# Expert feed-forward loops of a three-stage block: W1 slices as the stationary operand, the first norm's variance from matrix products

## The chip, the cores and the metric

The kernel runs on one core of a Trainium2 chip. The metric is device time in microseconds (us) of one execution; the time before is the median of three runs. Engines are named as the profile names them: PE (TensorE, with PEld for its weight loads), DVE (VectorE), ACT (ScalarE), POOL (GpSimd) and SP (SyncE, which here only issues transfers).

## The reference, cut to what matters

The block is x + 0.5 FFN(norm x), then x + attention(norm x), then x + 0.5 FFN(norm x) again, for 2048 tokens of 128 features. The FFN has eight experts, of which each token takes two:

```
h = jnp.einsum('td,edf->etf', xt, W1) + b1[:, None, :]
h = _layernorm(jax.nn.relu(h), g1, be1)
y = jnp.einsum('etf,efd->etd', h, W2) + b2[:, None, :]
y = _layernorm(jax.nn.relu(y), g2, be2)
...
out = jnp.einsum('te,etd->td', gate, y)
```

W1 is 128 x 512 per expert and W2 512 x 128. Everything is fp32.

## The kernel before

The program has three stages, f1 (first FFN, 46 to 160 us of the profiled span), the attention (160 to 337 us) and f2 (second FFN, 337 to 446 us, its first seven pairs woven into the attention's end by a written order). In each FFN stage tokens are sorted by expert into 39 tiles of 128 rows; a tile has one expert. The expert loop works on pairs of tiles, 20 per stage, n being the pair and u = n % 2 its buffer.

For a pair, PE turns the gathered rows (`turn_x`, line 963), multiplies the turned x by W1 (`hidden`, line 974: x stationary, 512 columns of W1 moving, the expert's place a register), turns relu's result in eight transposes (`turn_h`, line 983), and multiplies by W2 (`second`, line 993: turned h stationary, 128 columns of W2 moving, eight products per pair). The profile shows two records for each fp32 product. ACT copies x out of PSUM (line 749), makes the relu into `hh` (line 756), copies the turned h into `hT` (line 762), takes the two norms' square roots (`sqrt1` 766, `sqrt2` 770) and writes the scaled rows (`finish`, 777). DVE takes the mean and variance of the 512 hidden values with `stats1` (1378) and `moments1` (1385); W2's columns are centred beforehand, so that only the variance of the first norm is needed. It then makes r1 (`y_scale`, 1391), scales y and adds the bias (`y_sums`, 1397), takes the second norm's statistics (`y_stats`, 1403 to 1409) and applies it (`y_norm`, 1419 and 1421, behind `sqrt2`).

Each engine runs its queue in the order in which the code is written, and semaphores tie the queues. In a body of PE, `turn_h(n)`, `turn_x(n+2)`, `hidden(n+1)`, `second(n)` follow one another. On DVE, the statistics of pair n+1 stand between `y_stats` and `y_norm` of pair n-1. Pairs 2 to 7 of f1 and 6 to 15 of f2 are hardware loops with two pairs in an iteration, at whose head the expert numbers are loaded into registers; the others are written out. Pairs 8 to 19 of f1 carry work of the attention beside them (`between`, `behind`): pairs 8 to 11 a shared-bias product each on PE (1109) and an add on DVE. In f1, SP stores each finished pair (379), and after every second pair an empty 1032 KB block for f2 (426); POOL gathers the rows. In f2, SP loads each tile's rows (413) and POOL scatters the results.

## Time and profile before

| what | value |
|---|---|
| median of 3 runs (lowest to highest) | 470.97 us (470.0 to 471.98) |
| profiled execution: its own time, its span | 471.78 us, 469.6 us |
| PE busy, PEld busy | 406.1 us (86%), 282.9 us (60%) |
| DVE busy, ACT busy, POOL busy | 348.0 us (74%), 289.3 us (62%), 245.3 us (52%) |
| granted TensorE clock, mean | 0.926 |
| f1 / attention / f2 with the combination (from where the stages begin) | 46 to 160, 160 to 337, 337 to 470 us |

The span is the time from the first to the last instruction of the core; the execution's own time is 2.2 us longer. Busy shares are means over stages that have different limits, so an engine's need is to be read inside one stage. A start-to-start distance in a timeline is what an instruction costs its engine; its own length is up to 0.15 us longer, since the next one begins before it has ended.

### The profile page before, as it was taken

The numbers are of one execution on the slowest core, as the hardware profiler recorded it, in microseconds if no ns is written. First come the engines' busy times: TensorE is split into PE (matmuls) and PEld (weight loads), VectorE is DVE, ScalarE is ACT, GpSimd is POOL, SyncE is SP. The second block draws the span as 40 slices with busy tenths as digits, with TensorE's granted clock in tenths as the row PEclk, the third lists the DMA queues.
The fourth block names the chain that finished last, engine by engine and source line by source line (L and its number), as shares of the span: only waits on it lengthen the run. The fifth ranks groups of instructions, "written<-read, shape, count | busy, mean of one in ns | idle before, by whom it ended". The sixth has DMA issues, their size and how long they took to land.

```text
span 469.6 us, 11623 instructions
## 1 busy us (share of the span) xinstructions
PE 406.1 (86%) x3573; PEld 282.9 (60%) x3574; DVE 348.0 (74%) x1297; ACT 289.3 (62%) x594; POOL 245.3 (52%) x348
## 2 busy tenths in 40 slices
PE   7699999999798767888888998877889499999985
PEld 7445578777576544546465665644467278787734
DVE  8666678877749883789688797855668768888865
ACT  3186786765467765777576777743756357667630
POOL 8873643443631155366556757556624647555540
PEclk9798999999979955999799999978999889999998
DMA  7910116544433310000001000001111121211027
GB/s 214 338 65 17 29 48 214 175 155 141 137 76 122 131 35 22 21 13 24 13 18 24 19 26 24 25 29 34 53 47 35 55 53 53 62 57 55 30 75 228
DMA packets 27444, 35.15 MB, mean 75 GB/s; under 512 B 4329, under 2 KB 20641, under 8 KB 26242
## 3 DMA queue, kind: packets, MB, share of 16 engines
q1 hardware_dynamic: 22450, 24.62, 15.9%
q0 software_dynamic: 4944, 9.90, 7.7%
q8 instruction: 27, 0.44, 0.4%
q14 instruction: 23, 0.19, 0.1%
HBM read 15.45 MB, written 18.24 MB: 72 GB/s over the span
## 4 chain that ended last, share of the span: by engine, by line
PE 52%; DVE 15%; issue 10%; POOL 7%; ACT 7%; DMA 4%; another core or an unknown queue 2%; DVEq 1%; SPq 1%; POOLq 0%; ACTq 0%
PE bank L993 10%; PE bank L974 10%; PE bank L983 5%; DVE mx L2152 4%; PE bank L1915 2%; PE bank L1183 2%; PE bank L1178 2%; ACT early L1726 2%; PE bank L1933 2%; PE bank L2369 2%; PE bank L1937 2%; PE bank L1866 1%; PE bank L1935 1%; POOL xr_scratch L461 1%
## 5 line engine op out<-in xcount | busy, mean ns | idle before, releaser
L993 PEld LDWEIGHTS bank<-w2c,hT 128*128 128x128 f32 x624 | 77.4, 197 | 30.2 <-issue 29.1
L993 PE MATMUL bank<-w2c,hT 128*128 x624 | 78.9, 281 | 10.9 <-ACT hT L762 10.7
L974 PE MATMUL bank<-w1s,xT 128*128 x156 | 75.8, 608 | 0.8 <-DVE w2c L2387 0.8
L2152 DVE TENSOR_REDUCE mx<-bank 128x4 f32<-128x1024 f32 (+1 forms) x48 | 58.4, 1220 | 21.2 <-PE bank L1875 18.8
L1726 ACT ACTIVATE early<-bank 128x768 f32<-128x768 f32 x64 | 51.9, 813 | 30.4 <-PE bank L1923 29.9
L1378 DVE BATCH_NORM_STATS2 st<-wide 128x6 f32<-128x512 f32 x78 | 50.1, 683 | 22.8 <-ACT wide L756 12.7
L515 POOL DMA_INDIRECT xgw<-xn_scratch,slot_u x39 | 37.2, 954 | 45.3 <-PE bank L963 27.7
L762 ACT COPY hT<-bank 128x1024 f32<-128x1024 f32 (+1 forms) x40 | 39.5, 988 | 34.4 <-PE bank L983 30.5
L581 POOL DMA_INDIRECT yk<-y_scratch,posi x32 | 32.0, 1000 | 47.3 <-PE bank L1923 20.7
L485 POOL DMA_INDIRECT y_scratch<-yo,dest_u x39 | 39.0, 999 | 33.5 <-PE bank L983 19.4
L756 ACT ACTIVATE wide<-bank 128x1024 f32<-128x1024 f32 (+1 forms) x40 | 40.1, 1001 | 16.5 <-remote 7.1
L461 POOL DMA_INDIRECT xr_scratch<-row_buf,hi_i x32 | 31.7, 990 | 31.3 <-PE bank L1923 19.6
L983 PE MATMUL bank<-ident,wide 128*128 128x128 f32 x312 | 40.8, 273 | 1.3 <-issue 1.2
L974 PEld LDWEIGHTS bank<-w1s,xT 128*128 128x128 f32 x156 | 27.6, 194 | 22.8 <-issue 22.7
L983 PEld LDWEIGHTS bank<-ident,wide 128*128 128x128 f32 x312 | 35.1, 141 | 2.3 <-issue 2.0
L1915 PE MATMUL bank<-mxT,sel 64*128 64x384 bf16 x128 | 22.9, 354 | 12.8 <-ACT early L1726 6.8
L1397 DVE SCALAR_TENSOR_TENSOR yy<-bank,r,b2p 128x128 f32<-128x128 f32 x78 | 24.6, 351 | 11.2 <-remote 5.1
L939 ACT COPY wide<-bank 128x1024 bf16<-128x1024 bf16 x28 | 28.4, 1015 | 5.2 <-PE bank L1183 2.6
L777 ACT ACTIVATE yo<-yz,r 128x128 f32<-128x128 f32 x78 | 27.1, 396 | 3.6 <-DVE yz L1421 2.9
L1866 PE MATMUL bank<-mrhs,mlhs 64*128 64x128 bf16 (+1 forms) x192 | 16.7, 256 | 11.9 <-DVE mx L2152 7.2
L1915 PEld LDWEIGHTS bank<-mxT,sel 64*128 64x128 bf16 x128 | 6.3, 94 | 32.2 <-ACT early L1726 13.8
L1421 DVE SCALAR_TENSOR_TENSOR yz<-yy,mv,g2b 128x128 f32<-128x128 f32 x78 | 23.4, 340 | 0.2 <-issue 0.2
(382 smaller groups left out, 907.2 us busy)
## 6 DMA issues: line engine op xcount, KB each, us to landing
xr_scratch<-row_buf SPq DMA_DIRECT2D x8, 1032.0 KB
xgw<-xr_scratch SPq DMA_DIRECT2D x39, 64.5 KB
y_scratch<-yo SPq DMA_DIRECT2D x19, 128.0 KB
w1s<-in_L_ffn_W_dram SPq DMA_DIRECT2D x1, 2048.0 KB, 8.5
early<-y_scratch SPq DMA_DIRECT2D x8, 256.0 KB, 3.8
xs<-in_L_attn_x_dram SPq DMA_DIRECT2D x4, 256.0 KB, 3.6
xn_scratch<-row_buf SPq DMA_DIRECT2D x1, 1024.0 KB
out_dram<-xs SPq DMA_DIRECT2D x8, 128.0 KB, 2.5
```

The costliest lines, as they stand in the source:

```text
L461: pool.indirect_dma_start(out=xr_dram, out_offset=bass.IndirectOffsetOnAxis(ap=slot2[:, c:c + 1], axis=0), in_=rows_of[t // HALF][:, t % H ...
L485: pool.indirect_dma_start(out=y_dram, out_offset=bass.IndirectOffsetOnAxis(ap=dest_u[:, 2 * p + j:2 * p + j + 1], axis=0), in_=yo[:, p % 2 ...
L515: pool.indirect_dma_start(out=xg[:, u, :], out_offset=None, in_=xn_dram, in_offset=bass.IndirectOffsetOnAxis(ap=slot_u[:, n:n + 1], axis=0 ...
L756: act.activation(hh[:, u, 0:k, :], banks[:, h_at[u]:h_at[u] + k, :], ACT.Relu).then_inc(S["relu"], 1)
L762: act.copy(hT[:, u, 0:k, :], banks[:, 5:5 + k, :]).then_inc(S["hTc"], 1)
L974: last = pe.matmul(bank[h_at[u] + j][:], xT[:, u, j, :], w1s[:, bass.ds(e * FF, FF)], start=True, stop=True)
L983: last = pe.transpose(bank[5 + j][:, c * P:c * P + P], hh[:, u, j, c * P:(c + 1) * P], ident[:])
L993: last = pe.matmul(o[:, j * DIM:(j + 1) * DIM], hT[:, u, j, c * P:(c + 1) * P], w2c[:, bass.ds(e * (FC * DIM) + c * DIM, DIM)], start=(c = ...
L1378: last = dve.bn_stats(st1[:, u, j, :], hh[:, u, j, :])
L1726: act.activation(prob[:, g], quad[:, low:low + 2, 0:3 * P], ACT.Exp).then_inc(A["prob"], 1)
L1915: pe.matmul(o, sel[r:r + 64, g:g + 1].to_broadcast([64, P]), mxT[r:r + 64, :], start=True, stop=False)
L2152: dve.tensor_reduce(mx[:, c:c + 2 * per].rearrange("p (a q) -> p q a", q=2), quad[:, low:low + 2, :].rearrange("p q (a e) -> p q a e", a=p ...
```

## The change

`hidden` now keeps W1 stationary and moves x: four products of 128 columns per tile, so that h comes out turned and `turn_h`, `copy_hT` and the copy in `hh` are gone; relu writes `hT` itself. The stationary slices are read at fixed places: SP copies each tile's 256 KB of W1 from `w1s` to a buffer of two pairs (`stage_weights`, SBUF to SBUF, 78 copies in all), in f1 behind the store of the pair five before, in f2 behind the loads of the pair's rows, and PE waits for them. The first norm's variance now comes from two sums: W2 has a 129th column of ones, so that `second` also gives the sum of h, and the sum of squares comes from ACT (`square`, 1024 elements), DVE (`square_rows`, a reduction of the four 128-chunks to one) and PE (`square_sums`, a product with one moving column per tile). `variance` on DVE combines them in four instructions of one element per partition, after `second`, and `sqrt1` and `y_scale` follow. `stats1` and `moments1` are gone.

```diff
-        w2c = sb("w2c", [P, NE * FC * DIM])
+        w2c = sb("w2c", [P, NE * FC * ROW])
+        w2r = w2c[:].rearrange("p (a w) -> p a w", w=ROW)
...
-        hh = wide32[:].rearrange("p (u j f) -> p u j f", u=2, j=2)
+        early_w = early[:, 10 * DIM:10 * DIM + 4 * FF].rearrange("p (u j f) -> p u j f", u=2, j=2)
+        hs = early[:, 26 * DIM:30 * DIM].rearrange("p (u j e) -> p u j e", u=2, j=2)
+        hsq = wide32[:].rearrange("p (u j f) -> p u j f", u=2, j=2)
         hT = sb("hT", [P, 2, 2, FF])
-        st1 = sb("st1", [P, 2, 2, 6])
-        mv1 = sb("mv1", [P, 2, 2, 2])
...
+                sp.wait_ge(s_colc, 2 + NE)
+                sp.wait_ge(S["eid"], 1)
+                stage_weights(sp, S, 0)
+                stage_weights(sp, S, 1)
+                sp.wait_ge(s_w2g, 2)
+                sp.wait_ge(s_wmix, 2)
+                for p in range(2, 5):
+                    stage_weights(sp, S, p)
                 for p in range(PAIRS):
                     k = min(2, SLOT_TILES - 2 * p)
...
+                    if p + 5 < PAIRS:
+                        stage_weights(sp, S, p + 5)
...
                 sp.dma_start(xgw[:, n % 4, :], xr_dram[bass.ds(v, P), :]).then_inc(S[f"xg{n % 4}"], 16)
+                if n == 3:
+                    sp.wait_ge(S["eid"], 1)
+                    sp.wait_ge(A["qTp"], 2 * BATCH)
+                    sp.wait_ge(A["kTp"], 2 * BATCH)
+                    known = experts(sp, eid, 0, 4) + experts(sp, eid, 4, 8)
+                    stage_weights(sp, S, 0, known[0:2])
+                if n > 3 and (n % 2 or n == SLOT_TILES - 1):
+                    stage_weights(sp, S, p, known[2 * p:2 * p + 2] if p < AHEAD else ())
...
+        def weights_at(first, p):
+
+            if not first:
+                return (q6, k6)[p % 2][:].bitcast(F32).rearrange("p a s e -> p (a s e)").rearrange("p (j f) -> p j f", j=2)
+            return hsq[:, p] if p < 2 else early_w[:, p % 2]
...
+        def stage_weights(sp, S, p, known=()):
+
+            first = S is sems["f1"]
+            if p >= 2:
+                sp.wait_ge(S["h"], p - 1)
+            count = min(2, SLOT_TILES - 2 * p)
+            for j, e in enumerate(known or experts(sp, eid, 2 * p, count)):
+                sp.dma_start(weights_at(first, p)[:, j, :], w1s[:, bass.ds(e * FF, FF)]).then_inc(weights_staged(S, p % 2)[0], 16)
...
-            if isinstance(n, int) and n < AHEAD - 1:
-                return bank[7], 1
-            return bank[(7, 1)[u]], 2
+            return bank[(7, 5)[u]], 2
...
-                    act.wait_ge(S["hTp"], m - 1)
-                    act.wait_ge(S["bn"], m - 1)
-                act.activation(hh[:, u, 0:k, :], banks[:, h_at[u]:h_at[u] + k, :], ACT.Relu).then_inc(S["relu"], 1)
...
-            def copy_hT(n, u, k=2):
-                act.wait_ge(S["hTp"], n + 1)
-                if not (isinstance(n, int) and n < 2):
-                    act.wait_ge(S["A"], n - 1)
-                act.copy(hT[:, u, 0:k, :], banks[:, 5:5 + k, :]).then_inc(S["hTc"], 1)
+                    act.wait_ge(S["A"], m - 1)
+                act.activation(hT[:, u, 0:k, :], banks[:, h_at[u]:h_at[u] + k, :], ACT.Relu).then_inc(S["relu"], 1)
...
+            def square(m, u, k=2):
+                act.wait_ge(S["relu"], m + 1)
+                if not (isinstance(m, int) and m < 2):
+                    act.wait_ge(S["hss"], m - 1)
+                act.activation(hsq[:, u, 0:k, :], hT[:, u, 0:k, :], ACT.Square).then_inc(S["hsq"], 1)
...
-                act.activation(sd1[:, u, 0:k], mv1[:, u, 0:k, 1], ACT.Sqrt, bias=eps_c[:]).then_inc(S["sq1"], 1)
+                act.activation(sd1[:, u, 0:k], sd1[:, u, 0:k], ACT.Sqrt, scale=1.0 / FF, bias=eps_c[:]).then_inc(S["sq1"], 1)
...
-            def body(n, u, kx=2, kh=2, k=2, lag=2, beside=False):
-                copy_hT(n, u, k)
+            copy_xT, relu, square, sqrt1, sqrt2, finish = scalar_pair(act, S, first)
+
+            def body(n, u, kx=2, kh=2, lag=2, beside=False):
+                if kx:
+                    copy_xT(n + 2, u, kx)
+                if lag:
+                    sqrt1(n - 1, 1 - u)
                 if lag > 1:
                     finish(n - 2, u)
-                if kx:
-                    copy_xT(n + 2, u, kx)
                 if beside:
                     between(n - BESIDE)
                 if kh:
                     relu(n + 1, 1 - u, kh)
-                sqrt1(n, u, k)
                 if lag:
                     sqrt2(n - 1, 1 - u)
+                if kh:
+                    square(n + 1, 1 - u, kh)
...
-            def hidden(m, u, es):
+            def hidden(m, i, u, k):
+                first = S is sems["f1"]
                 pe.wait_ge(S["xTc"], m + 1)
+                staged, earlier = weights_staged(S, u)
+                pe.wait_ge(staged, i * 32 + earlier + 16 * k)
+                w = weights_at(first, m if isinstance(m, int) else 2 + u)
...
-                for j, e in enumerate(es):
-                    last = pe.matmul(bank[h_at[u] + j][:], xT[:, u, j, :], w1s[:, bass.ds(e * FF, FF)], start=True, stop=True)
-                last.then_inc(S["h"], 1)
-
-            def turn_h(n, u, k=2):
-                pe.wait_ge(S["relu"], n + 1)
-                if not (isinstance(n, int) and n == 0):
-                    pe.wait_ge(S["hTc"], n)
                 for j in range(k):
                     for c in range(FC):
-                        last = pe.transpose(bank[5 + j][:, c * P:c * P + P], hh[:, u, j, c * P:(c + 1) * P], ident[:])
-                last.then_inc(S["hTp"], 1)
-
-            def second(n, u, es):
-                pe.wait_ge(S["hTc"], n + 1)
+                        last = pe.matmul(bank[h_at[u] + j][:, c * P:(c + 1) * P], w[:, j, c * P:(c + 1) * P], xT[:, u, j, :],
+                                         start=True, stop=True)
+                last.then_inc(S["h"], 1)
...
+            def square_sums(n, u, k=2):
+                o = y_free(n, u)
+                pe.wait_ge(S["hsr"], n + 1)
+                for j in range(k):
+                    last = pe.matmul(o[:, 2 * ROW + j:2 * ROW + j + 1], hs[:, u, j, :], ones[:, 0:1], start=True, stop=True)
+                last.then_inc(S["hss"], 1)
...
+            def second(n, u, es):
+                o = y_free(n, u)
+                pe.wait_ge(S["relu"], n + 1)
                 for j, e in enumerate(es):
                     for c in range(FC):
-                        last = pe.matmul(o[:, j * DIM:(j + 1) * DIM], hT[:, u, j, c * P:(c + 1) * P],
-                                         w2c[:, bass.ds(e * (FC * DIM) + c * DIM, DIM)], start=(c == 0), stop=(c == FC - 1))
+                        last = pe.matmul(o[:, j * ROW:(j + 1) * ROW], hT[:, u, j, c * P:(c + 1) * P],
+                                         w2c[:, bass.ds(e * (FC * ROW) + c * ROW, ROW)], start=(c == 0), stop=(c == FC - 1))
                 last.then_inc(S["A"], 1)
...
-                turn_h(n, u, k)
                 if kx:
                 if kh:
-                    hidden(n + 1, 1 - u, e[2:2 + kh])
+                    hidden(n + 1, i + u, 1 - u, kh)
+                square_sums(n, u, k)
                 second(n, u, e[0:k])
...
-            def stats1(m, u, k=2):
-                dve.wait_ge(S["relu"], m + 1)
-                if not (isinstance(m, int) and m < 2):
...
+            def square_rows(m, u, k=2):
+                dve.wait_ge(S["hsq"], m + 1)
+                dve.tensor_reduce(hs[:, u, 0:k, :], hsq[:, u, 0:k, :].rearrange("p j (c e) -> p j e c", c=FC), X, ALU.add
+                                  ).then_inc(S["hsr"], 1)
+
+            def variance(m, u, k=2):
+                ls.start(m * PER + BEFORE)
+                dve.wait_ge(S["hss"], m + 1)
+                dve.wait_ge(S["A"], m + 1)
+                o = y_bank(S, m, u)[0]
                 for j in range(k):
-                    last = dve.bn_stats(st1[:, u, j, :], hh[:, u, j, :])
-                last.then_inc(S["bn"], 1)
-
-            def moments1(m, u, k=2):
-                dve.wait_ge(S["bn"], m + 1)
-                dve.memset(hold[:, 0:1], 0.0)
+                    total = o[:, j * ROW + DIM:(j + 1) * ROW]
+                    last = dve.tensor_scalar(r1[:, u, j:j + 1], total, total, 1.0 / FF, ALU.mult, ALU.mult)
+                ls(last)
                 for j in range(k):
-                    last = dve.bn_aggr(mv1[:, u, j, :], st1[:, u, j, :])
+                    q = r1[:, u, j:j + 1]
+                    last = dve.tensor_scalar(sd1[:, u, j:j + 1], o[:, 2 * ROW + j:2 * ROW + j + 1], q, q, ALU.max, ALU.subtract)
                 last.then_inc(S["mv1"], 1)
...
-            def body(n, u, es=None, k=2, kh=2, beside=False):
+            square_rows, variance, y_scale, y_sums, y_stats, y_norm = vector_pair(dve, S, LoopSteps)
+
+            def body(n, u, es=None, k=2, beside=False):
+                if es is not None:
+                    variance(n - 1, 1 - u, len(es))
+                square_rows(n, u, k)
                 if es is not None:
                     y_scale(n - 1, 1 - u, len(es))
-                moments1(n, u, k)
-                if es is not None:
                     y_sums(n - 1, 1 - u, es)
                     y_stats(n - 1, 1 - u, len(es))
                 if beside:
                     between(n - BESIDE)
-                if kh:
-                    stats1(n + 1, 1 - u, kh)
                 if es is not None:
                     y_norm(n - 1, 1 - u, es)
...
+            variance(PAIRS - 1, (PAIRS - 1) % 2, 1)
```

The written order of f2's first seven pairs is changed in the same sense (there `square_sums` stands behind `second`), and the POOL queue's waits for `hTp` become waits for `A`, the end of `second`.

Three places show it, all in the second pair of the iteration of f2's loop. On DVE, from the second norm's statistics (`st`, `mv`) of the pair before to that norm's application (`yz`), before:

```order
L100 REGISTER_ALU
L1407 MEMSET pads 1x1
L1409 BN_AGGR mv<-st 128x2 x2
L1374 REGISTER_ALU
L1378 BN_STATS st<-wide 128x6 x2
L1419 RECIPROCAL r<-sd 128x2
L1421 REGISTER_ALU
L1421 SCALAR_TENSOR_TENSOR yz<-yy,mv,g2b 128x128
```

and now:

```order
L100 REGISTER_ALU
L1462 MEMSET pads 1x1
L1464 BN_AGGR mv<-st 128x2 x2
L1474 RECIPROCAL r<-sd 128x2
L1476 REGISTER_ALU
L1476 SCALAR_TENSOR_TENSOR yz<-yy,mv,g2b 128x128
```

The two statistics of 512 values (`st<-wide`) that stood ahead of the reciprocal of the second norm are no longer there; the reciprocal follows the aggregation directly.

On DVE, the head of the body, from the reciprocal of the first norm (`r<-sd`) to the first scaled sum (`yy`), before:

```order
L1391 RECIPROCAL r<-sd 128x2
L1383 MEMSET pads 1x1
L1385 BN_AGGR mv<-st 128x2 x2
L100 ISA
L1397 REGISTER_ALU x2
L1397 ISA
L1397 SCALAR_TENSOR_TENSOR yy<-bank,r,b2p 128x128
```

and now:

```order
L1436 TENSOR_SCALAR r<-bank 128x1 x2
L100 ISA
L1440 TENSOR_SCALAR sd<-bank,r 128x1 x2
L1425 REGISTER_ALU
L1426 TENSOR_REDUCE early<-wide 128x256
L1446 RECIPROCAL r<-sd 128x2
L100 REGISTER_ALU
L1452 REGISTER_ALU x2
L1452 ISA
L1452 SCALAR_TENSOR_TENSOR yy<-bank,r,b2p 128x128
```

Four small instructions (`r<-bank`, `sd<-bank,r`, each twice) and the reduction of the squares (`early<-wide`) now stand ahead of that reciprocal, and the aggregation behind it is gone.

On PE, the body from its start to the products with W2, before:

```order
L983 MATMUL bank<-ident,wide 128x128 x8
L960 REGISTER_ALU
L962 ISA
L963 MATMUL bank<-ident,xgw 128x128 x2
L974 REGISTER_ALU x2
L974 ISA
L974 MATMUL bank<-w1s,xT 128x512
L974 REGISTER_ALU x2
L974 ISA
L974 MATMUL bank<-w1s,xT 128x512
```

and now:

```order
L1007 MATMUL bank<-ident,xgw 128x128 x2
L1014 ISA
L1018 REGISTER_ALU
L1023 MATMUL bank<-xT,k 128x128 x8
L1030 REGISTER_ALU
L1037 MATMUL bank<-ones,early 128x1 x2
L1045 REGISTER_ALU
L1045 ISA
L1045 MATMUL bank<-w2c,hT 128x129
```

Eight transposes are gone, two wide products have become eight of 128 columns from the staged slices (`k` is one of the buffers), and two products with one moving column (`ones`) stand between them and the products with W2.

## Rows read from the trace of the kernel before

**Rows 1.** Stretches: span, busy us (instructions) of PE, PEld, DVE, ACT, POOL; granted clock, DMA.
```profile
62.50:91.00 28.50, 28.50 (x190) 22.60 (x189) 24.15 (x106) 21.09 (x48) 11.31 (x12) 1.00 0.45 151
...
380.00:446.50 66.50, 65.33 (x430) 51.64 (x429) 53.76 (x246) 46.62 (x103) 40.01 (x55) 1.00 0.18 52
```

**Rows 2.** Timeline of PE, one pair of the second expert loop (start us, us).
```profile
408.06 1.04 PE L983 MATMUL bank<-ident,wide 128*128 128x128 f32 x8
...
408.93 0.38 PE L963 MATMUL bank<-ident,xgw 128*128 128x128 f32 x2
...
409.15 1.88 PE L974 MATMUL bank<-w1s,xT 128*128 x4
...
410.87 1.95 PE L993 MATMUL bank<-w2c,hT 128*128 x16
```

**Rows 3.** Timeline of DVE, same pair (in brackets: idle before, releaser).
```profile
407.53 1.29 DVE L1378 BATCH_NORM_STATS2 st<-wide 128x6 f32<-128x512 f32 x2 [0.59 <-ACT wide L756]
...
408.73 0.15 DVE L1419 RECIPROCAL r<-sd 128x2 f32<-128x2 f32 x1
...
409.31 0.16 DVE L1391 RECIPROCAL r<-sd 128x2 f32<-128x2 f32 x1
...
409.77 0.63 DVE L1397 SCALAR_TENSOR_TENSOR yy<-bank,r,b2p 128x128 f32<-128x128 f32 x2
...
411.38 0.15 DVE L1409 BATCH_NORM_AGGREGATE mv<-st 128x2 f32<-128x6 f32 x1
...
412.12 1.29 DVE L1378 BATCH_NORM_STATS2 st<-wide 128x6 f32<-128x512 f32 x2 [0.59 <-ACT wide L756]
```

**Rows 4.** Timeline of DVE, first expert loop, two heads of its iterations.
```profile
73.78 0.17 DVE L1391 RECIPROCAL r<-sd 128x2 f32<-128x2 f32 x1 [0.70 <-issue]
...
82.92 0.17 DVE L1391 RECIPROCAL r<-sd 128x2 f32<-128x2 f32 x1 [0.63 <-issue]
```

**Rows 5.** Timeline of PE, router products with few moving columns.
```profile
347.37 0.61 PE L640 MATMUL bank<-wrs,xnT 128*128 128x8 f32 x4
```

**Rows 6.** Groups of DVE by line and shape: busy us, mean ns.
```profile
L2152 DVE TENSOR_REDUCE mx<-bank 128x4 f32<-128x1024 f32 x32 | 38.9, 1220 | 12.2 <-PE bank L1875 12.1
...
L2107 DVE TENSOR_SCALAR ave<-amv 128x2 f32<-128x2 f32 x8 | 1.4, 170 | 0.3
...
L681 DVE TENSOR_REDUCE rank<-rank 128x8 bf16<-128x24 bf16 x8 | 1.4, 180 | 0.3
...
L1355 DVE TENSOR_REDUCE eidf<-yk 1x48 f32<-1x768 f32 x1 | 0.9, 941 | 0.0
...
L1332 DVE TENSOR_REDUCE posf<-gmix 128x32 f32<-128x256 f32 x1 | 0.4, 419 | 0.0
```

**Rows 7.** Timeline of DVE, last pairs of the second expert loop.
```profile
447.42 0.15 DVE L1409 BATCH_NORM_AGGREGATE mv<-st 128x2 f32<-128x6 f32 x1
...
447.93 0.17 DVE L1419 RECIPROCAL r<-sd 128x2 f32<-128x2 f32 x1 [0.36 <-ACT sd L770]
...
449.20 0.35 DVE L1397 SCALAR_TENSOR_TENSOR yy<-bank,r,b2p 128x128 f32<-128x128 f32 x1 [0.22 <-DVE r L1391]
```

**Rows 8.** Timeline of ACT, a relu in the second expert stage.
```profile
374.54 1.02 ACT L756 ACTIVATE wide<-bank 128x1024 f32<-128x1024 f32 x1 [7.13 <-remote]
```

**Rows 9.** DMA issues by line: KB each, us from issue to landing.
```profile
xr_scratch<-row_buf SPq DMA_DIRECT2D x8, 1032.0 KB
...
early<-y_scratch SPq DMA_DIRECT2D x8, 256.0 KB, 3.8
```

**Rows 10.** Timeline, first expert loop: a hidden product and a finished pair.
```profile
86.64 1.88 PE L974 MATMUL bank<-w1s,xT 128*128 x4
...
87.53 0.69 ACT L777 ACTIVATE yo<-yz,r 128x128 f32<-128x128 f32 x2
```

**Rows 11.** Timeline of PE, a pair that carries a shared-bias product.
```profile
91.24 1.02 PE L1109 MATMUL bank<-be2x,gsT 128*128 128x512 f32 x2
92.10 1.88 PE L974 MATMUL bank<-w1s,xT 128*128 x4
```

More of the change, by code:

```diff
@@ L778, in finish @@
                 last.then_inc(S["yf"], 1)
-            return copy_xT, relu, copy_hT, sqrt1, sqrt2, finish
+            return copy_xT, relu, square, sqrt1, sqrt2, finish
         def moe_scalar(act, S, first):
@@ L1052, in moe_tensor @@
             pe.wait_ge(S["eid"], 1 if first else 2)
-            turn_x, hidden, turn_h, second = tensor_pair(pe, S)
+            turn_x, hidden, square_sums, second = tensor_pair(pe, S)
             def body(n, i, u, e, kx=2, kh=2, k=2, beside=False):
-                turn_h(n, u, k)
                 if kx:
@@ L1699, in att_scalar @@
             F = sems["f2"]
-            copy_xT, relu, copy_hT, sqrt1, sqrt2, finish = scalar_pair(act, F, False)
+            copy_xT, relu, square, sqrt1, sqrt2, finish = scalar_pair(act, F, False)
             def half_values(s, seq):
@@ L2031, in output_products @@
                 last.then_inc(A["res"], 1)
-            turn_x, hidden, turn_h, second = tensor_pair(pe, F)
+            turn_x, hidden, square_sums, second = tensor_pair(pe, F)
             first_turn()
@@ L2050, in att_tensor @@
             turn_outputs(d, bank[1])
-            turn_h(1, 1)
+            square_sums(0, 0)
             turn_x(3, 1, 1)
@@ L2288, in att_vector @@
             turns(dve, turn)
-            stats1, moments1, y_scale, y_sums, y_stats, y_norm = vector_pair(dve, F, RunSteps)
+            square_rows, variance, y_scale, y_sums, y_stats, y_norm = vector_pair(dve, F, RunSteps)
             d = BATCH - 1
@@ L2297, in att_vector @@
             outputs(d)
-            stats1(0, 0)
+            square_rows(0, 0)
             mean_squares(d)
-            moments1(0, 0)
             batch_best(dve, F, step, d - 1)
@@ L2313, in att_vector @@
             batch_slots(dve, F, step, d - 1)
-            moments1(1, 1)
+            variance(1, 1)
             late_norm(dve, F, step, d)
+            square_rows(2, 0)
             y_scale(1, 1)
             y_sums(1, 1, e[2:4])
-            stats1(2, 0)
             y_stats(1, 1, 2)
@@ L2321, in att_vector @@
             batch_places(dve, F, step, d)
-            moments1(2, 0)
             y_norm(1, 1, e[2:4])
             batch_marks(dve, F, step, d)
+            variance(2, 0)
+            square_rows(3, 1)
             y_scale(2, 0)
```

135 lines of the change are left out of this document (69 added, 66 removed).

## Prediction

> **What bounds the kernel now.** I read the stretches of the profile first, because the mean shares mix three stages. In the two expert loops PE is busy for 28.50 of 28.50 us and for 65.33 of 66.50 us, at granted clock 1.00, the 2.4 GHz level, while DVE has 24.15 and 53.76 us and ACT 21.09 and 46.62 us [rows 1]. So PE is the bound there, but DVE stands at 85% and 81% of the same stretches. Whoever takes work from PE has only that distance to gain, and this change takes some of DVE's work away and gives it other work.
>
> The timeline of PE for one pair gives the price of each of its parts, start to start: `turn_h` 408.06 to 408.93 is .87 us, `turn_x` .22, `hidden` 1.72 [rows 2]. The pair's period is 412.12 - 407.53 = 4.59 us [rows 3], so `second` takes 4.59 - 2.81 = 1.78 for 16 records, .111 each. One such record is a product of a 128x128 fp32 weight with 128 columns in one of its two passes.
>
> The same pair on DVE gives the ring of that engine: `stats1` 407.53 to 408.73 is 1.20; `y_norm` to 409.31 is .58; from the first norm's reciprocal to `y_sums` (409.77) .46; from there to the end of the aggregation (411.38 + .15) 1.76 [rows 3]. That is 4.00 of work and .59 of waiting for ACT's relu. In the first loop DVE has no such wait but stands for .70 and .63 us at the head of each iteration of two pairs, with nothing else named as releaser [rows 4]: it loads registers there.
>
> **What the change costs and gives, per pair.** PE: `turn_h` goes (-.87). `hidden` becomes 8 products of 128 columns, 16 records at .111 = 1.78 instead of 1.72. `second` has 129 columns: 1.79. `square_sums` is new: two products, four records with one moving column. If such a record costs what a 128-column one costs, four are .44; the nearest rows with few columns, four records of 8 columns, were .61 long in all [rows 5], the other bound. I take .44, since a weight load of 128x128 must lie ahead of each in either form. The sum is .22 + 1.78 + .44 + 1.79 = 4.23, against 4.59: -.36 (bounds -.19 and -.40).
>
> DVE, one part after another, in the order that it now has:
> - `variance`: four instructions on one element per partition. An instruction on two elements is .17 long [rows 6], and a following one starts .08 earlier where nothing is in between, so the two pairs of them, the second waiting for the result of the first, are .25 + .04 + .25 - .08 = .46. Bounds: .34 (all four back to back) to .68 (none overlap).
> - `square_rows`: 256 results from 1024 elements. No such strided fp32 reduction is in the trace. Contiguous reductions: 128x1024 out of PSUM 1.220, 1x768 .941, 128x256 .419 [rows 6]; the last two give (941 - 419) / 512 = 1.02 ns for an element. I take 1.22, less .09 that the next start overlaps: 1.13 (bounds 1.05, the fitted line's 1.20 less .15, and 1.30).
> - from the reciprocal to `y_sums`: .46 now with an aggregation between them; without it the sum must wait for the reciprocal's result: a row of the end, where nothing stands between, shows .22 idle behind the .16 of the reciprocal [rows 7]. I take .42 (bounds .38 and .46).
> - `y_sums` to the aggregation's end: unchanged, 1.76.
> - the second norm's round trip: the reciprocal of `y_norm` needs `sqrt2` from ACT, which needs the aggregation. Today `stats1` with its 1.29 lies in that gap. With `stats1` gone nothing does. The trace shows the uncovered trip at the end of the loop: .36 idle on DVE, released by ACT's sd [rows 7]. I take .36; ACT's queue has relu ahead of `sqrt2`, but relu follows `hidden` and ends before that.
> - `y_norm` .63, its reciprocal no longer beside anything (bounds .58, .66).
>
> The sum is .46 + 1.13 + .42 + 1.76 + .36 + .63 = 4.76 (bounds 4.41 and 5.26). ACT gets `square` (1024 elements) for `copy_hT` (1024 elements) and is not the bound: relu of the same size is 1.02 [rows 8], and its 46.62 of 66.50 us are far from full [rows 1]. So **the bound moves from PE at 4.59 to DVE at 4.76**, +.17 for a pair; PE then has .53 of waiting per pair, which I expect ahead of `square_sums`. In the hardware loops the register loads at the head (.63 to .70 per two pairs, [rows 4]) come on top where no wait hides them: at most 4.76 + .33 = 5.09, and as part of them goes into the wait for `sqrt2` or ahead of it, I take 4.9, +.3 (PE's loop pays none of this).
>
> A rule of the Trainium skill speaks against `square_rows`. Its page "SBUF — State Buffer", section "Door 1: The DMA port swizzle (why `[64,N]` ≈ `[32,N]`)", says that a partition is read in cachelines of 16 bytes, that an access which goes on to another line pays a penalty, and that fp32 keeps its rate only for strides within four elements. Every element read here lies 512 bytes behind the one before. By that rule the reduction could take two steps for an element. The trace has one strided row, a reduction of 24 bf16 values to 8 with 16 bytes from one to the next: .180 [rows 6], and the contiguous line above gives .18 for 24 elements as well (419 - 232 x 1.02 = 182). The two agree to a few ns on 24 elements, so the trace so far does not bear the rule out, and I carry it as a rival.
>
> **The copies.** 78 copies of 256 KB are added. A 256 KB transfer into SBUF landed 3.8 us after its issue [rows 9]. In the first stage, the copy for pair 10 is asked for once pair 5 is stored: its `finish` ends at 87.53 + .69 = 88.22, and `hidden` of pair 10 starts two periods after the one at 86.64 [rows 10], at 95.8. Of these 7.6 us SP needs an estimated 2 for store, register loads and issues, the landing 3.8, and 1.8 is left. The DMA engines there have a busy share of .45 at 151 GB/s [rows 1]; 512 KB more per 4.6 us adds 114 GB/s, .34 by the same proportion. That is under 1, but the empty 1032 KB blocks [rows 9] stand in the same queue. In the second stage the share is .18 and the copies follow loads that are early already. I cost them at nothing but at the openings.
>
> **The sum.** Against the profiled execution's own 471.78 us: opening of the first stage, whose copies wait for W1 to be there and take 3.8, partly beside the rest of the preparation, +.5. Its six loop pairs at +.3: +1.8. Pairs 8 to 11, which carry a product of .86 (91.24 to 92.10, [rows 11]) on PE: PE now 4.23 + .86 = 5.09 instead of 5.45, DVE's add fills the .36 wait, so -.3 each, -1.2. Pairs 12 to 19 carry varied work on both engines: 0 (bounds ±2). End of the first stage, where `variance` and `sqrt1` now follow the last `second`: +.8. Second stage: its early pairs +1.0 (six at .17), thirteen later ones +2.2 (bounds +1 with less, +4 if the loop head costs here too), its end +.8. The relu of one pair there waits 7.13 us for the tokens' routing [rows 8]; that wait stands ahead of the change's work and I leave it (±4). Together .5 + 1.8 - 1.2 + .8 + 1.0 + 2.2 + .8 = +5.9: 477.7. The median is .8 below the profiled execution, so between 476.9 and 477.7; I say 477.5.
>
> **Rivals.**
> (1) Faster: DVE's ring turns out below PE's. The place is the gap between aggregation and `y_norm`: if the round trip to ACT costs nothing more than the small instructions around it, and `variance` is at its lower bound, DVE is at 4.41 - and with the .59 that it waits for ACT today gone, PE could set a period of 4.23. It decides where DVE falls under 4.59. With PE the bound, -.36 for some 25 pairs is -9.0, pairs 8 to 11 -1.4, openings and ends +2.1: 471.8 - 8.3 = 463.5. For it speaks that DVE's present ring has only 4.00 of work; against it, that `variance` and `square_rows` (1.59) replace the 1.20 of `stats1` and the part of `moments1` in the .46 and that the trip is measured at .36. Chance .22.
> (2) `square_rows` at two steps for an element: 1.20 + 1.07 more, DVE at 5.83. For 37 pairs 5.9 + 39.6: 517. Against it the strided row. Chance .08.
> (3) The copies come late in the first stage: the 1.8 us of slack goes if the 1032 KB block ahead takes its share. If each of 13 pairs then waits 1 us: 491. Chance .10.
> (4) Gains on PE and losses on DVE even out, for instance with a DVE ring at its middle between 4.41 and 4.76: 470 to 473. Chance .12.
> My forecast, 474 to 485: .48.
>
> **The numbers.** This kernel's measurement tells apart about 0.5%, which is 468.6 to 473.3. Faster takes rival 1 and a little of rival 4: .24. Same takes the rest of rival 4 and the low edge of the forecast: .16. Slower: .60. The range from 463 to 492 holds all but rival 2, the edge of rival 1 and some of rival 3; the likeliest case's own is 474 to 485.
>
> **What would show it.** A row of about 1.2 us for the reduction of squares (2.3 would be rival 2); some .36 idle on DVE ahead of the reciprocal of `y_norm`, released by ACT's sd; idle time on PE of about .5 ahead of the two one-column products, released by DVE; a period of 4.76 in the second loop and about 4.9 in the first; no wait of PE on a DMA in the steady pairs. A PE that is busy throughout at 4.23 would be rival 1. The prediction is wrong if `variance` is far from .46, if ACT's `sqrt2` stands behind relu, if the wait of 7.13 us moves, or if the clock falls below 1.00 in the loops because PE now waits.

## The result, and the profile after

The changed kernel takes 533.74 us (median of four runs, 526.64 to 536.66) against 470.83 us. Two of the four, the profiled one among them, were in a slower state and are left out of the ratio, 1.125 (95% interval 1.113 to 1.137); the other two average 529.77 us. The forecast of 477.5 had the sign and the engine, and lay 52 us below that; the range ended at 492. The profiled execution, the longest of the four, has a span of 534.3 us against 469.6 us.

The stages first, from the starts of the first `hidden` and the ends of the last `second` in the timelines of PE: the first stage went from 111.5 us (48.52 to 160.01) to 142.0 (49.17 to 191.14), the second from 106.9 (339.79 to 446.67) to 137.4 (374.69 to 512.14), and what lies between them from 179.8 to 183.6. So the two expert stages lost 30.5 us each, nearly all of the 64.7 of the span: 1.57 us on average for each of the 39 pairs that their 78 tiles make.

The stretches of the changed kernel (columns as in [rows 1]):

```profile
62.50:91.00 28.50, 21.14 (x177) 20.15 (x177) 22.61 (x77) 15.97 (x35) 8.48 (x9) 0.99 0.45 161
...
424.00:512.00 88.00, 66.76 (x515) 63.24 (x515) 70.55 (x242) 46.08 (x98) 39.23 (x54) 0.95 0.31 107
```

PE is no longer busy throughout: 21.14 of 28.50 us and 66.76 of 88.00, where before it was 28.50 of 28.50 and 65.33 of 66.50. DVE now stands ahead of it, but is not full either: it too waits. Two pairs on DVE in the second loop show for what (columns as in [rows 3]):

```profile
471.00 0.35 DVE L1436 TENSOR_SCALAR r<-bank 128x1 f32<-128x1 f32 x2
...
477.56 0.35 DVE L1436 TENSOR_SCALAR r<-bank 128x1 f32<-128x1 f32 x2 [0.66 <-issue]
477.95 0.46 DVE L1440 TENSOR_SCALAR sd<-bank,r 128x1 f32<-128x1 f32 x2
478.33 1.91 DVE L1426 TENSOR_REDUCE early<-wide 128x256 f32<-128x1024 f32 x1
480.16 0.16 DVE L1446 RECIPROCAL r<-sd 128x2 f32<-128x2 f32 x1
480.54 0.63 DVE L1452 SCALAR_TENSOR_TENSOR yy<-bank,r,b2p 128x128 f32<-128x128 f32 x2 [0.22 <-DVE r L1446]
...
482.15 0.15 DVE L1464 BATCH_NORM_AGGREGATE mv<-st 128x2 f32<-128x6 f32 x1
482.75 0.17 DVE L1474 RECIPROCAL r<-sd 128x2 f32<-128x2 f32 x1 [0.45 <-ACT sd L810]
482.86 0.62 DVE L1476 SCALAR_TENSOR_TENSOR yz<-yy,mv,g2b 128x128 f32<-128x128 f32 x2
483.39 0.35 DVE L1436 TENSOR_SCALAR r<-bank 128x1 f32<-128x1 f32 x2
```

From 477.56 to 483.39 is one ring: 5.83 us, against 4.00 of work before [rows 3]. `variance` (lines 1436 and 1440) is .77, the reduction of the squares 1.83 start to start, the way to `y_sums` .38, from there to the end of the aggregation 1.76, the wait for `sqrt2` .45, the norm .64. Ahead of the first row stand .66 that nothing but DVE's own issue accounts for: the head of an iteration. The pair before, which has that gap in it, was 6.56 long (471.00 to 477.56), so two pairs take 12.39, 6.20 each. The rows of PE that answer to [rows 2] show the other side:

```profile
480.39 0.58 PE L1037 MATMUL bank<-ones,early 128*128 128x1 f32 x4 [1.38 <-DVE early L1426]
480.83 2.04 PE L1045 MATMUL bank<-w2c,hT 128*128 x16
482.70 0.38 PE L1007 MATMUL bank<-ident,xgw 128*128 128x128 f32 x2
482.92 1.95 PE L1023 MATMUL bank<-xT,q 128*128 128x128 f32 x16
486.22 0.58 PE L1037 MATMUL bank<-ones,early 128*128 128x1 f32 x4 [1.35 <-DVE early L1426]
```

PE waits 1.38 and 1.35 us for the reduction in these two pairs, at the place that was forecast (.53 there). Its own parts came out as they were costed: the two one-column products .44, `turn_x` .22, `second` 1.87 where 1.79 was taken. The waits of PE, summed, carry the same name (us in total, times, longest):

```profile
PE bank L1037 <- DVE early L1426: 42.3, 28, 3.7
```

### The profile page after: what moved, and what is told of

Read it like the earlier page. It is cut to its first block, busy times and chain, and to the rows that moved or that the text cites. A ratio compares the mean times of both kernels' runs of the same rounds, so it can differ in the third digit from the quotient of the medians.

```text
span 534.3 us, 12524 instructions
## 1 busy us (share of the span) xinstructions
PE 417.4 (78%) x3881; PEld 326.5 (61%) x3886; DVE 398.1 (75%) x1297; ACT 293.6 (55%) x594; POOL 245.8 (46%) x349
## 4 chain that ended last, share of the span: by engine, by line
DVE 31%; PE 25%; issue 19%; ACT 8%; DMA 4%; POOL 4%; DVEq 3%; SPq 2%; another core or an unknown queue 2%; POOLq 0%; ACTq 0%
DVE early L1426 5%; DVE mx L2204 4%; PE bank L1045 4%; PE bank L1023 3%; DVE sd L1440 2%; PE bank L1234 2%; DVE r L1436 2%; DVE yy L1452 2%; DVE st L1460 2%; DMA early<-y_scratch 2%; PE bank L1969 1%; DVE yz L1476 1%; ACT wide L983 1%; PE bank L1987 1%
## 5 line engine op out<-in xcount | busy, mean ns | idle before, releaser
L1045 PE MATMUL bank<-w2c,hT 128*128 x624 | 90.2, 303 | 0.1
L1426 DVE TENSOR_REDUCE early<-wide 128x256 f32<-128x1024 f32 (+1 forms) x40 | 74.8, 1870 | 3.8 <-ACT wide L802 3.8
L2204 DVE TENSOR_REDUCE mx<-bank 128x4 f32<-128x1024 f32 (+1 forms) x48 | 58.4, 1221 | 21.0 <-PE bank L1929 21.0
L1037 PE MATMUL bank<-ones,early 128*128 128x1 f32 x156 | 23.1, 251 | 45.4 <-DVE early L1426 42.3
L1037 PEld LDWEIGHTS bank<-ones,early 128*128 128x128 f32 x156 | 21.7, 200 | 50.4 <-issue 50.4
L796 ACT ACTIVATE hT<-bank 128x1024 f32<-128x1024 f32 (+1 forms) x40 | 39.6, 990 | 19.0 <-PE bank L1023 11.2
L810 ACT ACTIVATE sd<-mv,eps_c 128x2 f32<-128x2 f32 (+1 forms) x40 | 11.8, 295 | 60.4 <-DVE mv L1464 52.4
L802 ACT ACTIVATE wide<-hT 128x1024 f32<-128x1024 f32 (+1 forms) x40 | 40.9, 1022 | 0.0
L1023 PE MATMUL bank<-xT,early 128*128 128x128 f32 x280 | 38.2, 295 | 1.3 <-ACT hT L796 1.3
L1023 PEld LDWEIGHTS bank<-xT,early 128*128 128x128 f32 x280 | 36.9, 210 | 3.7 <-issue 3.4
L1452 DVE SCALAR_TENSOR_TENSOR yy<-bank,r,b2p 128x128 f32<-128x128 f32 x78 | 24.6, 351 | 10.6 <-DVE r L1446 9.8
L1436 DVE TENSOR_SCALAR r<-bank 128x1 f32<-128x1 f32 x78 | 13.8, 218 | 20.4 <-issue 11.7
```

Of the source, the lines that this page charges most:

```text
L796: act.activation(hT[:, u, 0:k, :], banks[:, h_at[u]:h_at[u] + k, :], ACT.Relu).then_inc(S["relu"], 1)
L802: act.activation(hsq[:, u, 0:k, :], hT[:, u, 0:k, :], ACT.Square).then_inc(S["hsq"], 1)
L1023: last = pe.matmul(bank[h_at[u] + j][:, c * P:(c + 1) * P], w[:, j, c * P:(c + 1) * P], xT[:, u, j, :], start=True, stop=True)
L1037: last = pe.matmul(o[:, 2 * ROW + j:2 * ROW + j + 1], hs[:, u, j, :], ones[:, 0:1], start=True, stop=True)
L1045: last = pe.matmul(o[:, j * ROW:(j + 1) * ROW], hT[:, u, j, c * P:(c + 1) * P], w2c[:, bass.ds(e * (FC * ROW) + c * ROW, ROW)], start=(c = ...
L1426: dve.tensor_reduce(hs[:, u, 0:k, :], hsq[:, u, 0:k, :].rearrange("p j (c e) -> p j e c", c=FC), X, ALU.add).then_inc(S["hsr"], 1)
```

## The experiments

The theory after the result: DVE's ring sets the period in both loops, and three of its terms were too small: the reduction (1.83 for 1.13), `variance` (.77 for .46) and the loop's head (.33 per pair and more, taken at 0 to .14). The rivals: the added copies hold the loops back; or PE does, and DVE's rows are only where the time shows. Each kernel was timed beside the kernel before on the same chip, and the chips differ. So what a change gave is taken here as the difference of two ratios times 470 us, with the 95% interval that follows from theirs. Where that interval reaches to zero, only the rows of the trace can tell.

One stretch serves to compare the traces: pairs 6 to 15 of the second stage, from the end of one `second` on PE to the end of the tenth after it. It took 46.2 us before and 62.0 in the changed kernel, 6.20 for a pair. Code is cut to the lines that matter, and `...` stands for what is left out.

**e1: the squares written so that the reduction reads them in a row.**

```
-act.activation(hsq[:, u, 0:k, :], hT[:, u, 0:k, :], ACT.Square)
+act.activation(hsq[...].rearrange("p j (e c) -> p j c e", c=FC), hT[...].rearrange("p j (c e) -> p j c e", c=FC), ACT.Square)
-dve.tensor_reduce(..., hsq[...].rearrange("p j (c e) -> p j e c", c=FC), ...)
+dve.tensor_reduce(..., hsq[...].rearrange("p j (e c) -> p j e c", c=FC), ...)
```

> ACT writes the squares with the four chunks side by side (stride of 16 bytes on its output), so that the reduction on DVE reads its 1024 elements in a row. Theory (DVE's ring of variance .77, reduction 1.83, sums and statistics 2.2, round trip .36 and norm .73 sets the period, 6.20 us with the loop head): if the distance of 512 bytes makes the reduction 1.92 long, the row falls to about 1.25, the period by .67, and the time by 39 x .67 = 26 us to about 508. If the 256 results of four elements each are what costs, the row stays at 1.9 and the time at 534. ACT's square may become longer than 1.02; up to 2 us it stays hidden. Rival (the added copies, not DVE, hold the loops back): the time stays at 534 even where the row gets shorter.

Measured: 518.94 us, ratio 1.106 (1.098 to 1.113), 9 us less (±7). The groups of ACT and DVE by line and shape:

```profile
L802 ACT ACTIVATE wide<-hT 128x1024 f32<-128x1024 f32 x38 | 78.1, 2056 | 0.0
L1426 DVE TENSOR_REDUCE early<-wide 128x256 f32<-128x1024 f32 x38 | 46.1, 1214 | 13.1 <-ACT wide L802 11.5 <-issue 1.6
```

The reduction of the same 1024 elements into the same 256 results is now 1.214 instead of 1.915 long: the distance between the elements cost .70, not their number. Of the 26 us only a third came. A part of the rest is seen: the strided write makes ACT's square 2.06 long (1.04 in the changed kernel), and DVE waits 11.5 us for it in all, where it waited 3.8. That ACT would hide it up to 2 us was wrong. The ten pairs of the second stage take 57.0 us, .49 less for each where .67 was expected. That a shorter row on DVE took time off speaks against both rivals.

**e2: two additions instead of the reduction.**

```
-dve.tensor_reduce(hs[:, u, 0:k, :], hsq[...].rearrange("p j (c e) -> p j e c", c=FC), X, ALU.add).then_inc(S["hsr"], 1)
+dve.tensor_tensor(hsq[..., 0:half], hsq[..., 0:half], hsq[..., half:FF], ALU.add).then_inc(S["hsr"], 1)
+dve.wait_ge(S["hsr"], 2 * m + 1)
+dve.tensor_tensor(hs[:, u, 0:k, :], hsq[..., 0:P], hsq[..., P:half], ALU.add).then_inc(S["hsr"], 1)
```

> Two contiguous additions (512 and 256 elements per partition) on DVE take the place of the reduction. Theory: additions of this shape were .68 and are estimated at .36 for half, with a wait between them about 1.1 instead of 1.83: period -.7, time 39 x .7 = 27 us less, about 506. Rival (copies): 534.

Measured: 506.80 us, ratio 1.079 (1.072 to 1.086), 21 us less (±7), which holds the theory's 27 at its edge. The timeline of DVE:

```profile
435.62 0.46 DVE L1442 TENSOR_SCALAR sd<-bank,r 128x1 f32<-128x1 f32 x2
436.00 0.68 DVE L1427 TENSOR_TENSOR wide<-wide 128x512 f32<-128x512 f32 x1
436.72 0.42 DVE L1429 TENSOR_TENSOR early<-wide 128x256 f32<-128x256 f32 x1
437.06 0.16 DVE L1448 RECIPROCAL r<-sd 128x2 f32<-128x2 f32 x1
```

The sums take 1.06 (436.00 to 437.06) in place of 1.83, and the ten pairs of the second stage 53.9 us, .81 less for each.

**e3: the reduction left out.** `square_sums` reads the first 128 squares, `hsq[:, u, j, 0:P]`, as soon as ACT has written them, and `square_rows` is empty.

> The reduction is left out and PE sums the squares of the first 128 hidden values alone (so the norm uses a wrong variance). Theory: 1.83 goes from DVE's ring, but the wait for sqrt1 is uncovered (+.4): ring 5.85 - 1.4 = 4.45, with the loop head 4.8, so 39 x 1.4 = 55 us less: about 479. Rival (PE would be the bound at 4.23 as soon as the reduction is gone): 470 or below. Rival (copies): above 510.

Measured: 489.34 us, ratio 1.039 (1.029 to 1.049): 40 us less (±7), where the theory had 55, and far from the 470 of a PE that is the bound at 4.23. So the reduction was the largest part, and without it the ring is still too long. DVE now waits ahead of the first norm's reciprocal also, and the loop's head is there (.97 at 427.28). The timeline of DVE:

```profile
422.89 0.17 DVE L1444 RECIPROCAL r<-sd 128x2 f32<-128x2 f32 x1 [0.36 <-ACT sd L806]
```

**e4: small copies.**

```
-sp.dma_start(weights_at(first, p)[:, j, :], w1s[:, bass.ds(e * FF, FF)])
+n = FF if p < 4 else 8
+sp.dma_start(weights_at(first, p)[:, j, 0:n], w1s[:, bass.ds(e * FF, n)])
```

> From the fifth pair of a stage on, a copy of W1 moves 4 KB instead of 256 KB per tile, so that the products use old weights (wrong results); the waits stay. Theory: the time stays within 1% of 533.7, DVE sets the period. Rival (copies late or in the way of the engines): 20 us or more less.

Measured: 527.32 us (523.42 to 536.90), ratio 1.124 (1.117 to 1.131), beside 1.125: 1 us less (±7). The copies' traffic is worth at most some 7 us here; the rival's 20 or more is out. The trace of the changed kernel says the same: PE waits 2.6 us in all for copies of W1, in three places, and all three are openings of a stage. In e4 the ten pairs of the second stage still take 61.3 us.

**e5: a shorter variance, on top of e2.**

```
-    last = dve.tensor_scalar(r1[:, u, j:j + 1], total, total, 1.0 / FF, ALU.mult, ALU.mult)
-ls(last)
-for j in range(k):
-    q = r1[:, u, j:j + 1]
-    last = dve.tensor_scalar(sd1[:, u, j:j + 1], o[:, 2 * ROW + j:2 * ROW + j + 1], q, q, ALU.max, ALU.subtract)
+    last = dve.tensor_scalar(r1[:, u, j:j + 1], total, total, -1.0 / (FF * FF), ALU.mult, ALU.mult)
...
+    last = act.activation(sd1[:, u, j:j + 1], o[:, 2 * ROW + j:2 * ROW + j + 1], ACT.Sqrt, scale=1.0 / FF, bias=r1[:, u, j:j + 1])
```

> On top of e2: variance is two instructions on DVE without a wait between them (minus the squared mean of each tile), and ACT's square root subtracts it as its bias and reads the sum of squares itself (two instructions of one element; epsilon comes in with the second addition, the clamp at zero is left out). Theory (DVE's ring sets the period): variance falls from .77 to about .35, so 39 x .42 = 16 us less than e2: about 490. Rival (ACT's longer square root, or PE, takes over): 500 or above.

Measured: 494.41 us, ratio 1.054 (1.047 to 1.061), 12 less than e2 (±5) where 16 were expected. In the timeline of DVE `variance` is down from .77 to .26 (437.56 to 437.82), and the wait behind the statistics is as before:

```profile
436.92 0.17 DVE L1474 RECIPROCAL r<-sd 128x2 f32<-128x2 f32 x1 [0.45 <-ACT sd L813]
437.03 0.61 DVE L1476 SCALAR_TENSOR_TENSOR yz<-yy,mv,g2b 128x128 f32<-128x128 f32 x2
437.56 0.35 DVE L1440 TENSOR_SCALAR r<-bank 128x1 f32<-128x1 f32 x2
437.82 0.68 DVE L1430 TENSOR_TENSOR wide<-wide 128x512 f32<-128x512 f32 x1
```

**e6: the round trip covered, on top of e5.** In a body of DVE `add_quarters(n)` (the second addition) stands behind `y_stats(n - 1)`; in a body of PE the two products change places:

```
-square_sums(n, u, k)
 second(n, u, e[0:k])
+square_sums(n, u, k)
```

> On top of e5: of the two additions the second stands behind the second norm's statistics, where DVE waits for ACT's square root, and PE's product with the ones stands behind the products with W2. Theory: the idle .36 ahead of the norm is filled, ring .35 + .68 + .42 + 1.76 + .42 + .63 = 4.26, with the loop head 4.6, near PE's 4.23: 39 x .36 = 14 us less than e5, about 476. Rival (the new chain, second addition to product to variance, waits as long as was gained): 490.

Measured: 493.40 us, ratio 1.049 (1.039 to 1.058), no less than e5 as far as the intervals tell (2 less, ±5): the theory's 14 us didn't come. In the traces the second stage got shorter than in e5 (119.2 to 113.6 us) and the first longer (120.8 to 125.4). The timeline of PE in the second loop shows what stands against the gain:

```profile
433.09 0.43 PE L1010 MATMUL bank<-ident,xgw 128*128 128x128 f32 x2 [0.83 <-issue]
433.37 1.99 PE L1026 MATMUL bank<-xT,k 128*128 128x128 f32 x16
435.19 1.95 PE L1048 MATMUL bank<-w2c,hT 128*128 x16
436.98 0.50 PE L1040 MATMUL bank<-ones,early 128*128 128x1 f32 x4
437.35 0.41 PE L1010 MATMUL bank<-ident,xgw 128*128 128x128 f32 x2
```

From 433.09 to 437.35 is 4.26, the pair that the prediction had for PE alone (4.23). But at an iteration's head PE now stands .83. A reading that e6 doesn't test: what PE waits for is the last thing in the body, so only .4 us of products are queued when it goes on to the register loads.

**e7: DVE's expert numbers loaded late, on top of e6.** The numbers are read behind `variance` and the first addition:

```
-e = experts(dve, eid, i * 4 - 2, 4)
+e = []
 for u in range(2):
-    body(i * 2 + u, u, e[2 * u:2 * u + 2])
+    body(i * 2 + u, u, e[2 * u:2 * u + 2], load=None if u else lambda: e.extend(experts(dve, eid, i * 4 - 2, 4)) or e[0:2])
```

> On top of e6: DVE loads the expert numbers not at the head of an iteration but behind variance and the first addition, so that the register loads run while these two are at work. Theory: the .7 us of idle time per iteration (16 pairs in loops, and four more heads) falls by about .5: 10 x .5 = 5 us less than e6, about 471, and PE becomes the bound in the loops. Rival (the idle time at the head is the loop's jump or a wait for PE): no change against e6.

Measured: 493.86 us, ratio 1.047 (1.037 to 1.058): no change where 5 us were expected. In e6 DVE stood only 4.7 us ahead of `variance` by its own issue, and PE 7.4 us at its heads. That PE's heads were the bound there is a reading; e11 tests it. This miss doesn't speak on DVE's head in the changed kernel; e10 does.

**e8: no wait for `sqrt2`.** In `y_norm` of the changed kernel, `dve.reciprocal(r2, sd2)` becomes `dve.reciprocal(r2, mv2[..., 1])`, and the wait for ACT becomes one for DVE's own aggregation.

> The changed kernel, whose second norm takes the reciprocal of the variance instead of that of ACT's square root (wrong scale), so that DVE doesn't wait for ACT ahead of it. Theory: the uncovered round trip of .36 to .45 per pair goes: 39 x .36 = 14 us less, about 520. Rival (the wait is only the place where DVE would stand anyway): 534.

Measured: 519.99 us, ratio 1.112 (1.105 to 1.119), 6 less (±7) where 14 were expected: as a time, not told from nothing. The trace tells more:

```profile
437.55 0.15 DVE L1464 BATCH_NORM_AGGREGATE mv<-st 128x2 f32<-128x6 f32 x1
437.82 0.17 DVE L1474 RECIPROCAL r<-mv 128x2 f32<-128x2 f32 x1
```

The gap behind the aggregation is .12, where the trip left .45 and .36, and the ten pairs of the second stage take 58.4 us, .36 less for each. So the uncovered trip is on the path there, at about its own length.

**e9: other distances.** The reduction takes four elements 8 bytes apart in the first stage and 16 bytes apart in the second:

```
+hsq[:, u, 0:k, :].rearrange("p j (a c b) -> p j a b c", c=FC, b=2 if S is sems["f1"] else 4)
```

> The reduction of the changed kernel sums other elements (wrong sums): in the first expert stage four elements that stand 8 bytes apart, in the second stage four that stand 16 bytes apart, each into one of 256 results; the same count of elements and results as with 512 bytes apart (1.92) and side by side (1.21). If the rate depends on whether the next element lies within 16 bytes, as the Trainium skill's page SBUF - State Buffer (Door 1) has it, the row is about 1.2 at 8 and at 16 bytes, or 1.9 at 16 bytes if four elements on is already another line; if any distance costs, it is 1.9 at both.

One execution, 528.09 us; the rows of DVE's timeline are what counts, one of each stage:

```profile
73.75 1.21 DVE L1426 TENSOR_REDUCE early<-wide 128x256 f32<-128x1024 f32 x1
...
436.26 1.96 DVE L1426 TENSOR_REDUCE early<-wide 128x256 f32<-128x1024 f32 x1
```

8 bytes apart costs nothing (1.21, as side by side in e1), 16 bytes apart costs as much as 512 (1.96 and 1.92). The Trainium skill's page "SBUF — State Buffer", section "Door 1: The DMA port swizzle (why `[64,N]` ≈ `[32,N]`)", says that a line of 16 bytes needs two hits for the full rate, and that agrees. Its second step, that fp32 may stride by four elements for nothing, doesn't: at four elements, 16 bytes, the price is there.

**e10: DVE's expert numbers loaded late, in the changed kernel.** The edit of e7 alone, with the reduction in the place of the addition.

> The changed kernel, whose DVE loads the expert numbers not at an iteration's head but behind variance and the reduction are issued. Theory (the register loads stand uncovered at the head, .7 us per two pairs in 16 pairs and at some heads of written-out pairs): they run beside the reduction, 10 x .6 = 6 us less, about 528. Rival (the idle time is the jump or a wait for PE): 534.

Measured: 522.66 us, ratio 1.111 (1.102 to 1.120), 7 less (±7) where 6 were expected: as a time, hardly told from nothing. The waits of DVE ahead of `variance` that nothing but issue accounts for (us in total, times, longest), in the changed kernel and in this one:

```profile
DVE r L1436 <- issue: 11.7, 13, 3.2
```

```profile
DVE r L1436 <- issue: 0.5, 2, 0.2
```

The gap is gone with the place of the loads, so it was theirs and not the jump's. In the first loop six pairs took 40.29 us in the changed kernel (67.28 to 107.57, from one start of `variance` to another), 6.72 each, with gaps of 1.46, 1.39 and 1.00 at the three heads and one wait of 1.14 for `second` that is not of this kind. Here six take 35.25 (67.10 to 102.35), 5.88 each, about the ring of 5.83 alone. In the second stage the ten pairs take 58.9 us, .31 less for each.

**e11: PE's numbers late too, on top of e7.** The loads stand ahead of `second` (`e = load()`), and `sqrt1` ahead of `copy_xT` on ACT.

> On top of e7: PE too loads the expert numbers only ahead of the products with W2, and ACT takes the first norm's square root ahead of the copy of the turned x. Theory: in e7 PE stood .7 to 1.0 us at the head of each iteration, since the product that it waited for stood last in the body; this goes, 8 to 10 pairs-of-two x .8 = 8 us less than e7: about 485. In the loops the period is then near PE's 4.3. Rival: the wait is for something else, 493.

Measured: 493.79 us, ratio 1.050 (1.045 to 1.054): no change again. PE's gap by issue ahead of `turn_x` went from 7.9 us in 13 places (e7) to 1.6 in 3, and in its place PE waits for rows (4.5 us in six places):

```profile
429.91 0.33 PE L1010 MATMUL bank<-ident,xgw 128*128 128x128 f32 x1 [0.75 <-DMA xgw<-xr_scratch]
430.10 2.05 PE L1026 MATMUL bank<-xT,k 128*128 128x128 f32 x16
```

In the second loop nine periods take 43.32 us (405.94 to 449.26), 4.81 each. So PE's heads alone were not what held e6 and e7.

**e12: e11 with the small copies of e4.**

> On top of e11: from the fifth pair of a stage on a copy of W1 moves 4 KB instead of 256 KB per tile (old weights, wrong results); the waits and the number of issues stay. In e11 PE waited for the gathered rows in the second stage, at a period of 4.9 instead of the 4.3 of its own work. Theory (the copies cost nothing while DVE sets the period, but take time from the rows' loads, which stand behind them in SP's queue, once it is short): the waits for the rows go and the second stage's loop comes near 4.4 per pair, 10 us less than e11, about 484. Rival (the rows wait for POOL or for SP's issues): no change, 492 to 495.

Measured: 481.66 us, ratio 1.027 (1.020 to 1.033), 11 less than e11 (±4). The sum is what the theory gave, the place is not: nine periods of the second loop still take 42.06 us (401.76 to 443.82), 4.67 each, so the loop gave 1.3 us there, and one wait for rows remains in most of its iterations. So the copies' traffic does cost once the ring is short, about 11 us over the program, where e4 showed 1 (±7), but what else holds the rows back in the second loop (POOL's scatter or SP's issues) was not taken apart.

## Why the prediction was wrong

**What held.** PE's side: `turn_h` and the copy gone, the two one-column products at .44, `hidden` and `second` at their sums; e6 shows the pair of 4.26 that was forecast as 4.23. The bound moves to DVE. `square_rows` shows as the row ahead of which DVE hardly waits (3.8 us in all, for ACT) and behind which PE waits. The round trip to ACT's `sqrt2` is uncovered, .36 to .45 a pair, and without it e8's ten pairs are .36 shorter each. `y_sums` to the aggregation stayed 1.76. The copies don't decide (e4), and no steady pair waits for one.

**The step that failed** is the choice of 1.13 for `square_rows`, "bounds 1.05 and 1.30", with the Trainium skill's rule on lines of 16 bytes set aside because a strided row of 24 elements agreed with the contiguous line [rows 6]. The row could not tell: the price that e1 shows is (1.915 - 1.214) / 1024 = .68 ns per element, 16 ns on 24 elements, which a line drawn through two rows of other shapes cannot resolve. The bound from below and above came from contiguous rows alone, so the true 1.83 lay outside. Rival 2, which took the rule at two steps for an element, had the place right and the row too long (2.3), and its chance of .08 was too low. Its ring of 5.83 is the measured one to the digit, but by luck: it put all of the 1.07 above 4.76 into the reduction, which has .70 of it, while .31 is in `variance` and the rest in the trip and small terms.

**Two terms beside it** were mis-sized. `variance` measured .77 (bounds .34 and .68). Its first pair of instructions, whose result the second needs, takes .39 from start to start (477.56 to 477.95) where .29 was taken (.25 and .04 of waiting), and the second pair .38 where .17 was. In e5 the first pair, followed by an addition that doesn't need it, takes .26, as the two-element row [rows 6] had let expect; so .13 of the .39 is the wait for the result. Why the second pair takes .38 was not tested. e5 takes .51 out and gives 12 us. And the head of an iteration costs DVE .66 to .74 in the second stage, .33 and more per pair, and .80 to 1.46 in the first. The forecast gave it .14 per pair in the first stage and nothing in the second, where only the upper bound (+4) held it: the .59 of waiting that hid it before [rows 3] had gone with the bound's move, and this was not carried to the second stage. e10 shows it in the trace, the waits by issue down from 11.7 us to .5; as a time it is 7 us (±7).

Together, for a pair of the second loop: 4.76 + .70 + .31 + .33 + .04 (the trip) = 6.14, and 6.20 is measured, 1.61 over the 4.59 before. Taken out by themselves, the reduction gave 21 us (e2) and the long `variance` 12 (e5). Over 39 pairs the 1.61 would be 62.8, near the 61.1 that the two stages lost, but that nearness is luck. By the ends of `second` in the timelines of PE, the stretches lost quite different amounts:

| stage, pairs | before | changed | lost | forecast |
|---|---|---|---|---|
| first, 2 to 7 (loop) | 27.7 | 40.0 | 12.4 | 1.8 |
| first, 8 to 11 | 22.7 | 27.6 | 4.9 | -1.2 |
| first, 12 to 19 | 47.0 | 57.6 | 10.6 | 0 (±2) |
| second, 1 to 5 | 34.9 | 43.7 | 8.8 | 1.0 (six pairs) |
| second, 6 to 15 (loop) | 46.2 | 62.0 | 15.7 | 2.2, with the next row |
| second, 16 to 19 | 15.5 | 23.4 | 8.0 | |

In e4's trace pairs 8 to 11 take 24.5, so a part of their 4.9 belongs to this execution. Pairs 12 to 19 of the first stage, which carry the attention's work and were given 0 (±2) without a sum, are a term that missed by some 10 us, and not by the reduction: e3, which has none, still takes 54.8 us there. DVE waits 11.2 us for ACT's square roots in these pairs of e3, but what sets their pace was not tested.

PE's granted clock, 1.00 in both loops before, was .95 in the second loop (424 to 512 us) and .88 in the first stage from 91 to 190 us, where PE was busy 79% of the time; what it cost was not tested apart.

The opening of the second stage was given nothing, and its first `hidden` waits 2 us for its copy:

```profile
374.69 2.02 PE L1023 MATMUL bank<-xT,q 128*128 128x128 f32 x16 [2.03 <-DMA q<-w1s]
```

SP issues that copy at 371.87, behind the loads of the first four tiles' rows (from 367.58); the attention's last use of the buffer on PE lies 36 us earlier (335.7). How much of the 3.8 us that the stretch between the stages grew is this wait can't be told: with the same wait there, that stretch takes 175.6 us in e8 and 182.8 in e10.

One slip of the prediction's sums changed nothing: with the terms as given, the bounds of DVE's ring come out as 4.47 and 5.22, not 4.41 and 5.26.

**What stays open.** No version here beats the kernel before. From e5 on each wait that was taken away turned up in another engine: PE's head, then the rows' loads, and in the first stage the attention's work between the pairs, which with `square_sums` now stands between PE and its next product. That last one was only read from e7's timeline and not tested. With it stays open what pairs 12 to 19 of the first stage pay for.

## What to carry to other kernels

A rule that speaks against an edit is to be tested against a row that can show its size: work out first how long the row would be by the rule, and whether that differs by more than the rows scatter; if not, the rule stays in the range. When the bound moves to an engine, whatever its waits used to hide (a loop's head, a round trip to another engine) has to be added to its ring in the same step, in every stage. A reduction over a long distance is better done by additions of whole blocks, 1.06 against 1.83 us here.

## What the runs showed of the hardware

A reduction of 1024 fp32 elements per partition into 256 took 1.21 us with the elements side by side or 8 bytes apart, 1.96 at 16 bytes and 1.92 at 512 bytes. On ACT, writing 1024 fp32 elements 16 bytes apart took 2.06 us instead of 1.02 to 1.04. At the heads of the loops, where the expert numbers are loaded into registers, DVE stood .66 to 1.46 us in the changed kernel; with the loads behind the reduction (e10) it stood .5 us over the whole program. PE stood .83 and .74 us at two such heads in e6.
